# Five whole-tile slots filled by half-tile transfers, later stores, and a 512-column bias in a two-layer graph kernel

## The reference, cut to what matters

```python
# layer 0
x_norm = layernorm(x, g_in, b_in)
logits = x_norm @ Wn + bn;  gumbel = -log(-log(clip(u)) + EPS)
gate = straight_through(softmax(logits + gumbel))[:, 1]
view1 = x_norm
view2 = (adj * gate[:, None] * gate[None, :]) @ x_norm
g = sigmoid(concat([view1, view2], -1) @ Wg + bg)
fused = g * (view1 @ W1 + b1) + (1.0 - g) * (view2 @ W2 + b2)
x = layernorm(x + layernorm(fused + x, g_out, b_out))
# layer 1 (hyperbolic)
xt = logmap0(mobius_add(mobius_matvec(weight, x), expmap0(bias)))
h = adj @ xt
x = layernorm(x + hyperbolic_relu(h))
```

## Time and profile before

| | |
|---|---|
| median of 3 runs | 1006.14 us (1006.14 to 1008.36) |
| the profiled execution | 1008.98 us, span 1007.2 us |
| mean granted TensorE clock | 0.979 |
| busy, share of the span | PE 92%, DVE 79%, ACT 69%, GpSimd 22% |
| 16 DMA engines busy with the kernel's own queue | 75.4% |
| read from HBM, written | 271.37 MB, 9.46 MB |

### The profile page before, as it was taken

How to read it: one execution, slowest core, us unless ns; L and a number is a source line. 1 busy time by engine, 2 the same in 40 slices (tenths; PEclk the granted TensorE clock), 3 DMA queues, 4 the chain that set the end, 5 groups by cost and what they waited for, 6 DMA issues and landing times.

```text
span 1007.2 us, 12535 instructions
## 1 busy us (share of the span) xinstructions
PE 926.0 (92%) x4020; PEld 724.4 (72%) x4020; DVE 794.3 (79%) x1769; ACT 693.5 (69%) x1233; POOL 225.5 (22%) x201
## 2 busy tenths in 40 slices
PE   3888899999999999999999999998998988889983
PEld 2444677777878787878787887876777766668772
DVE  3555789888898979697784858669998887889984
ACT  4676476868686767656573654667878877778883
POOL 2220111121111111111010201002003716264552
PEclk8999999999999999999999999999999999999997
DMA  7677597977777677768584655758999897999890
GB/s 263 232 269 246 229 374 291 342 283 293 292 282 293 261 292 255 288 217 326 190 312 161 234 191 211 273 184 288 347 347 355 329 354 296 362 352 364 334 355 21
DMA packets 51537, 281.65 MB, mean 280 GB/s; under 512 B 6496, under 2 KB 8080, under 8 KB 20368
## 3 DMA queue, kind: packets, MB, share of 16 engines
q1 hardware_dynamic: 51472, 280.86, 75.4%
HBM read 271.37 MB, written 9.46 MB: 279 GB/s over the span
## 4 chain that ended last, share of the span: by engine, by line
PE 52%; DVE 20%; DMA 8%; ACT 8%; POOL 7%; issue 3%; SPq 1%; POOLq 0%; ACTq 0%; DVEq 0%
PE PS L982 15%; PE PS L984 15%; PE PS L983 15%; DMA A<-in_adjT_dram 6%; DVE AL L744 4%; DVE XGL L744 4%; DVE XTL L744 3%; PE PS L1066 2%; PE PS L1063 2%; DVE BS L693 2%; PE PS L980 1%; DMA xnt_scratch<-XNT 1%; ACT XGH L566 1%; POOL SINV L492 1%; ACT AH L566 1%
## 5 line engine op out<-in xcount | busy, mean ns | idle before, releaser
L744 DVE TENSOR_TENSOR AL<-A,AH 128x1024 fp32r<-128x1024 f32 x272 | 323.9, 1220 | 35.8 <-ACT AH L566 34.5
L566 ACT ACTIVATE AH<-A 128x1024 fp32r<-128x1024 f32 x272 | 277.2, 1057 | 88.8 <-PE PS L984 54.3
L982 PE MATMUL PS<-AH,XTH 128*128 128x512 f32 x326 | 131.7, 404 | 16.9 <-DVE AL L744 16.8
L982 PE MATMUL PS<-AH,XGH 128*128 128x512 f32 x364 | 145.4, 400 | 1.4 <-DVE AL L744 1.3
L984 PE MATMUL PS<-AH,XGL 128*128 128x512 f32 x364 | 141.8, 390 | 0.0
L983 PE MATMUL PS<-AL,XGH 128*128 128x512 f32 x364 | 141.7, 389 | 0.0
L744 DVE TENSOR_TENSOR XGL<-A,XGH 128x1024 fp32r<-128x1024 f32 x108 | 126.5, 1218 | 14.0 <-ACT XGH L566 13.8
L983 PE MATMUL PS<-AL,XTH 128*128 128x512 f32 x326 | 128.9, 395 | 0.0
L984 PE MATMUL PS<-AH,XTL 128*128 128x512 f32 x326 | 128.7, 395 | 0.0
L566 ACT ACTIVATE XGH<-A 128x1024 fp32r<-128x1024 f32 x108 | 107.9, 1053 | 17.4 <-DMA A<-in_adjT_dram 17.3
L469 POOL TENSOR_TENSOR r_rs<-r_v,NHALF 128x4 f32<-128x4 f32 x24 | 44.5, 1855 | 268.1 <-DVE r_v L699 268.1
(11 more groups left out here) (229 smaller groups left out, 1525.9 us busy)
## 6 DMA issues: line engine op xcount, KB each, us to landing
A<-in_adjT_dram SPq DMA_DIRECT2D x243, 1024.0 KB, 6.3
XR<-in_x_dram SPq DMA_DIRECT2D x16, 256.0 KB, 5.4
GB<-gate_scratch SPq DMA_DIRECT2D x12, 256.0 KB, 4.8
XNT<-xnt_scratch SPq DMA_DIRECT2D x12, 256.0 KB, 5.0
x_scratch<-X SPq DMA_DIRECT2D x12, 256.0 KB, 7.4
xnt_scratch<-XNT SPq DMA_DIRECT2D x6, 256.0 KB, 4.0
xnt_scratch<-X1T SPq DMA_DIRECT2D x6, 256.0 KB, 4.5
FU<-in_x_dram SPq DMA_DIRECT2D x4, 256.0 KB, 5.1
```

The lines of the kernel that those rows point to most:

```text
L566: a.activation(high(m), A[:, n % RING, h * HW:(h + 1) * HW], ACT.Copy).then_inc(S["hi"], 1)
L744: v.tensor_tensor(low(m), A[:, n % RING, h * HW:(h + 1) * HW], high(m).bitcast(F32), ALU.subtract).then_inc(S["lo"], 1)
L982: p.matmul(acc, hi[:, st], high(m)[:, mv], start=start, stop=False)
```

## The change

RING goes from 4 to 5 and SPLITS from 5 to 4. `load_a` moves each tile by two transfers of half a tile (4 KB in each partition), each half of a slot with a semaphore of its own (ld0a, ld0b, ...); the transfer of a half waits only for the same half of the slot's earlier tile, and ScalarE (TensorE for the unsplit tiles) waits for each half apart. The stores of results and the reloads of residuals move two tiles later in SyncE's queue. In the epilogue of layer 0 the columns are put in another order (V1 part first), the biases become 512 columns wide (a fourth part holds b1/2), and from row block 4 on view2 is no longer multiplied by -W2/2: the columns hold V1/2, the gate's argument and V2. VectorE computes (1 + tanh) * V1/2, (tanh - 1) * V2 and the difference of halves instead, which is one operation more.

```diff
-RING = 4
-SPLITS = 5
+RING = 5
+SPLITS = 4
+SUBTRACT_ON_DVE = 4
+STORE_AFTER = 15
+RELOAD_AFTER = 4
@@ load_a
-                if n >= RING:
-                    if n - RING in WHOLE:
-                        sp.wait_ge(S["used"], 2 * (n - RING + 1))
-                    else:
-                        sp.wait_ge(S["lo"], SPLIT_COUNT[2 * (n - RING) + 1])
                 row = (c * NCH + q) * P
-                sp.dma_start(A[:, n % RING, :], adjT[row:row + P, :]).then_inc(S[f"ld{n % RING}"], 16)
+                for h, name in enumerate("ab"):
+                    if n >= RING:
+                        if n - RING in WHOLE:
+                            sp.wait_ge(S["used"], 2 * (n - RING) + h + 1)
+                        else:
+                            sp.wait_ge(S["lo"], SPLIT_COUNT[2 * (n - RING) + h])
+                    sp.dma_start(A[:, n % RING, h * HW:(h + 1) * HW],
+                                 adjT[row:row + P, h * HW:(h + 1) * HW]).then_inc(S[f"ld{n % RING}{name}"], 16)
@@ start of the queue
-            for t, v in ((HB[:, :], b_hyp), (B3[:, 0:P], bg), (B3[:, P:2 * P], b1), (B3[:, 2 * P:3 * P], b2),
+            for t, v in ((HB[:, :], b_hyp), (B4[:, 0:P], b1), (B4[:, P:2 * P], bg), (B4[:, 2 * P:3 * P], b2), (B4[:, 3 * P:], b1),
                          (GOUT[:, :], g_out), (BOUT[:, :], b_out)):
@@ loop of the queue
                 for o, end in enumerate(ENDS):
-                    if n == end // 2 + 13:
+                    if n == end // 2 + STORE_AFTER:
                         store(o)
-                    if n == end // 2 + 2:
+                    if n == end // 2 + RELOAD_AFTER:
                         reload(o)
                 load_a(n)
@@ split_high
-                if h == 0:
-                    act.wait_ge(S[f"ld{n % RING}"], 16 * (n // RING + 1))
+                act.wait_ge(S[f"ld{n % RING}{'ab'[h]}"], 16 * (n // RING + 1))
@@ VectorE, fuse
+                    if front >= SUBTRACT_ON_DVE:
+                        link(v.scalar_tensor_tensor(out=v4(TH[:, :]), in0=v4(TH[:, :]), scalar=-1.0, in1=E[:, :, 2 * P:3 * P],
+                                                    op0=ALU.add, op1=ALU.mult))
+                        link(v.scalar_tensor_tensor(out=FU[:, :], in0=TH[:, :], scalar=-0.5, in1=FU[:, :],
+                                                    op0=ALU.mult, op1=ALU.add))
+                    else:
+                        link(v.tensor_tensor(v4(FU[:, :]), v4(FU[:, :]), E[:, :, 2 * P:3 * P], ALU.add))
@@ TensorE, l0
-                        p.matmul(E[:, t, 0:3 * P], ones[:, :], BP[:, :], start=True, stop=False)
+                        if front >= SUBTRACT_ON_DVE:
+                            p.matmul(E[:, t, P:3 * P], ones[:, :], BP[:, P:3 * P], start=True, stop=False)
+                            p.matmul(E[:, t, 0:P], ones[:, :], BP[:, 3 * P:], start=False, stop=False)
+                        else:
+                            p.matmul(E[:, t, 0:3 * P], ones[:, :], BP[:, 0:3 * P], start=True, stop=False)
                         p.matmul(E[:, t, 0:2 * P], XNT[:, blk(t)], RX[:, :], start=False, stop=False)
-                        last = p.matmul(E[:, t, 0:3 * P], GB[:, blk(t)], RS[:, :], start=False, stop=True)
+                        right = slice(P if front >= SUBTRACT_ON_DVE else 0, 3 * P)
+                        last = p.matmul(E[:, t, right], GB[:, blk(t)], RS[:, right], start=False, stop=True)
```

More of the change, by code:

```diff
@@ L163, in build @@
         BNB = sb("BNB", [P, 2])
-        BP = sb("BP", [P, 3 * P], BF16)
-        BR = sb("BR", [P, 3 * P], BF16)
+        BP = sb("BP", [P, CW], BF16)
+        BR = sb("BR", [P, CW], BF16)
         ones = sb("ones", [P, P], BF16)
@@ L168, in build @@
         NEG = sb("NEG", [P, BLK])
-        B3 = PART[:, 0, 0:3 * P]
+        B4 = PART[:, 0, :]
         WH = PART[:, 1, 0:P]
@@ L207, in build @@
         for name in (
-                "ld0", "ld1", "ld2", "ld3", "hi", "lo", "used",
+                "ld0a", "ld0b", "ld1a", "ld1b", "ld2a", "ld2b", "ld3a", "ld3b", "ld4a", "ld4b",
+                "hi", "lo", "used",
                 "xin0", "xin1", "xin2", "urow", "norm_vecs", "weights", "vecs", "const", "ident_ready",
@@ L379, in _ @@
             sp.dma_start(HBC[:, :], b_hyp.rearrange("(p o) -> p o", o=1)).then_inc(S["vecs"], 16)
-            for t, v in ((RX[:, 0:P], wg[0:P, :]), (RX[:, P:2 * P], w1), (RS[:, 0:P], wg[P:2 * P, :]),
-                         (RS[:, P:2 * P], w2), (RS[:, 2 * P:3 * P], w2), (WH, w_hyp)):
+            for t, v in ((RX[:, 0:P], w1), (RX[:, P:2 * P], wg[0:P, :]), (RS[:, 0:P], w2),
+                         (RS[:, P:2 * P], wg[P:2 * P, :]), (RS[:, 2 * P:3 * P], w2), (WH, w_hyp)):
                 sp.dma_start(t, v).then_inc(S["weights"], 16)
@@ L419, in _ @@
             for o, end in enumerate(ENDS):
-                if end // 2 + 2 >= NT:
+                if end // 2 + RELOAD_AFTER >= NT:
                     reload(o)
             for o, end in enumerate(ENDS):
-                if end // 2 + 13 >= NT:
+                if end // 2 + STORE_AFTER >= NT:
                     store(o)
@@ L569, in hyp_setup @@
                 if k == 1:
[L570 removed]
+                    act.wait_ge(S["vecs"], 128)
                     a.activation(JUNK[:, 0:P], HB[:, :], ACT.Square, accum_out=hbs[:, 0:1]).then_inc(S["hb_sq"], 1)
@@ L748, in prepare @@
                 dve.wait_ge(S["weights"], 16 * 6)
-                v.tensor_scalar(RX[:, P:2 * P], RX[:, P:2 * P], 0.5, None, ALU.mult)
-                v.tensor_scalar(RS[:, P:2 * P], RS[:, P:2 * P], -0.5, None, ALU.mult).then_inc(S["wt_scaled"], 1)
-                dve.wait_ge(S["vecs"], 112)
+                v.tensor_scalar(RX[:, 0:P], RX[:, 0:P], 0.5, None, ALU.mult)
+                v.tensor_scalar(RS[:, 0:P], RS[:, 0:P], -0.5, None, ALU.mult).then_inc(S["wt_scaled"], 1)
+                dve.wait_ge(S["vecs"], 128)
                 dve.wait_ge(S["const"], 1)
-                link(v.tensor_tensor(B3[:, P:2 * P], B3[:, P:2 * P], B3[:, 2 * P:3 * P], ALU.subtract))
-                link(v.tensor_scalar(B3[:, P:2 * P], B3[:, P:2 * P], 0.5, None, ALU.mult))
+                link(v.tensor_tensor(B4[:, 0:P], B4[:, 0:P], B4[:, 2 * P:3 * P], ALU.subtract))
+                v.tensor_scalar(B4[:, 0:P], B4[:, 0:P], 0.5, None, ALU.mult)
+                link(v.tensor_scalar(B4[:, 3 * P:], B4[:, 3 * P:], 0.5, None, ALU.mult))
                 for row in (0, 32):
-                    v.tensor_copy(BP[row:row + 1, :], B3[row:row + 1, :])
-                    link(v.tensor_copy(BR[:, :], B3[:, :]))
-                    link(v.tensor_tensor(B3[:, :], B3[:, :], BR[:, :], ALU.subtract))
-                v.tensor_copy(BP[64:65, :], B3[64:65, :]).then_inc(S["bias_ready"], 1)
+                    v.tensor_copy(BP[row:row + 1, :], B4[row:row + 1, :])
+                    link(v.tensor_copy(BR[:, :], B4[:, :]))
+                    link(v.tensor_tensor(B4[:, :], B4[:, :], BR[:, :], ALU.subtract))
+                v.tensor_copy(BP[64:65, :], B4[64:65, :]).then_inc(S["bias_ready"], 1)
             stats_pre(0)
@@ L839, in first @@
                     dve.wait_ge(S["tanh"], front + 1)
-                    link(v.scalar_tensor_tensor(out=v4(FU[:, :]), in0=v4(TH[:, :]), scalar=1.0,
-                                                in1=E[:, :, P:2 * P], op0=ALU.add, op1=ALU.mult))
-                    link(v.tensor_tensor(v4(FU[:, :]), v4(FU[:, :]), E[:, :, 2 * P:3 * P], ALU.add))
+                    link(v.scalar_tensor_tensor(out=v4(FU[:, :]), in0=v4(TH[:, :]), scalar=1.0, in1=E[:, :, 0:P],
+                                                op0=ALU.add, op1=ALU.mult))
+                    if front >= SUBTRACT_ON_DVE:
+                        link(v.scalar_tensor_tensor(out=v4(TH[:, :]), in0=v4(TH[:, :]), scalar=-1.0, in1=E[:, :, 2 * P:3 * P],
+                                                    op0=ALU.add, op1=ALU.mult))
+                        link(v.scalar_tensor_tensor(out=FU[:, :], in0=TH[:, :], scalar=-0.5, in1=FU[:, :],
+                                                    op0=ALU.mult, op1=ALU.add))
+                    else:
+                        link(v.tensor_tensor(v4(FU[:, :]), v4(FU[:, :]), E[:, :, 2 * P:3 * P], ALU.add))
                     if front >= ADD_ON_PE:
```

7 lines of the change are left out of this document (3 added, 4 removed).

## The result

The changed kernel takes **995.36 us** (median of 4 runs, 994.71 to 995.79) where the kernel before takes 1007.25 (1006.14 to 1009.46): a ratio of 0.9879, with a 95% interval of 0.9858 to 0.9899. That is faster, by 11.9 us or 1.2%. The forecast was 989 us in a range of 976 to 1001. The profiled execution took 994.71 us with a span of 992.9, 14.3 less than the profiled one of before; this is the pair that the forecast's sum of -17.2 is to be held against term by term. It flatters the change: the profiled execution of before is slower than its median, and that of the change is the fastest of its four. By the medians the forecast of 989 is 6.4 us too low.

What follows compares the result with a forecast made beforehand. The prediction took TensorE to bound 375 to 670 us, VectorE 670 to 750, and late loads behind store waits 750 to 981. Its terms summed to -17.2 us, giving 989 us from 1006.14, range 976 to 1001.

Steps and rivals of the forecast that it cites:

- The last stretch: 750 to 981 us: a DMA share of 0.965, smaller packets, earlier loads and less cover for GpSimd together give -9.9 us.
- Start: Start of the kernel: five more issues ahead of the first x_norm store delay ScalarE's next step, +1.2 us (0 to +2.4).
- Gate rows: Store of the gate rows: the load ahead of it waits for an earlier tile, -2.5 us (0 to -4.5).
- 110 to 375 us: Loads come sooner with five slots and halves, partly offset by fewer homes and load_front: -2 us (-5.5 to +2).
- Rival E: Row blocks 10 and 11: the missing home starves TensorE, some 30 us lost, slower at 1019 us; chance 0.05.
- Epilogue on TensorE: Row blocks 4 to 11: 128 fewer float32 columns per matmul, less 32 extra bf16 matmuls, -5.9 us (-3.3 to -6.8).
- Epilogue on VectorE: One more 512-column operation eight times, +0.7, and splits entering 670 to 750 us later, 1.2: +1.9 us (0 to +4).
- Homes from 375 us on: Row blocks 10 and 11 keep four homes; they refill while TensorE works on others: 0 us (0 to +5).
- B: Only TensorE's share comes; 750 to 981 us brings nothing: -7.3 us, 999 us; chance 0.17.
- C: 750 to 981 us reaches TensorE's limit, 25 us come back instead of 9.9: 974 us; chance 0.08.
- F: The whole kernel: the terms cancel within 3 us, 1006 us; chance 0.04.
- D: After 750 us small transfers lower the full-share DMA rate, deciding from 343 GB/s; 1016 us at 330; chance 0.04.

Runs made afterwards that it cites:

- experiment 2: The changed kernel with stores and reloads back at their old places in SyncE's queue, five slots and halves kept: 1000.16 us, ratio 0.9919.
- experiment 4: The changed kernel with four slots and five homes (RING = 4, SPLITS = 5), half transfers and late stores kept: 999.87 us, ratio 0.9918.
- experiment 6: The changed kernel with four slots (RING = 4) and its four homes, half transfers and late stores kept: 1004.98 us, ratio 0.9966.
- experiment 3: The changed kernel with one transfer and one semaphore for a whole tile, five slots and late stores kept: 996.52 us, ratio 0.9886.
- experiment 5: The kernel before with only stores and reloads moved two tiles later; four slots, five homes, whole transfers, old epilogue: 1005.45 us, ratio 0.9971.
- experiment 12: The changed kernel with four slots, five homes and the old places of stores and reloads; halves and 512-column epilogue kept: 1006.21 us, ratio 0.9969.
- experiment 1: The changed kernel with all 384 columns of the fp32 matmul back in every epilogue and no subtraction on VectorE: 998.4 us, ratio 0.9904.
- experiment 7: The changed kernel with load_front one tile later (k = 11 instead of 10), where it stood in time before: 993.5 us, ratio 0.9864.
- experiment 9: The changed kernel with early homes kept until row blocks 6, 8, 10 and 12 instead of 6, 6, 10 and 10: 991.34 us, ratio 0.9846.

## Why the prediction was right, and where it was not

The sign, the range and the place were right: most of the gain lies in the last stretch, and it comes from loads issued in time. Taken out of the change alone, the late stores cost 4.8 us there (experiment 2), the fifth slot 1.9 to 3.5 (experiments 4 and 6), the halves nothing (experiment 3). The sum was 2.9 us too good for the profiled pair, and that closeness is luck in part: the terms were 8.3 us too pessimistic in three places (gate rows, VectorE, last stretch) and 11.2 us too good in the others, the last half included. Term by term, by positions:

**The last stretch: forecast -9.9, measured -12.9, with 1.1 coming back in the last half.** The share I took, 0.965, came out at 0.96, the rate of a full share at 374 GB/s for 371, the packets at 8 ns for 9. What I had wrong is how the parts add. Gains of this stretch in the traces:

```
late stores alone                      -3.0   (experiment 5)
halves alone                           -5.4   (experiment 12)
halves and late stores, four homes     -9.3   (experiment 6)
halves and late stores, five homes    -11.0   (experiment 4)
halves and fifth slot, stores old      -8.1   (experiment 2)
fifth slot and late stores            -12.9   (experiment 3)
all                                   -12.9   (the change)
```

The forecast gave the halves 3.2 us of margin, the slot its own, the stores theirs, as if each was worth something in the presence of the others. Halves and late stores together are more than their sum, 11.0 against 8.4. As I read the waits, the chain needs both gone: halves alone leave 29.0 us of store waits, late stores alone leave ScalarE 25.6 us of waits for tiles, both leave 16.3. The difference of 2.6 us is larger than the 1.8 by which kernels with the same last part differ, but not by much. By the ratios late stores are worth 0.0051 with halves (experiments 12 and 4) and 0.0029 without (experiment 5), and their intervals do not part the two. The fifth slot with a home less adds 1.9; with four homes on either side (experiment 6) it adds 3.5. Once it is there, the halves add nothing. The last finding is against the title: the half-tile transfers are the part that this kernel could do without. All but its first row keep the 512-column epilogue; without it (experiment 1) the stretch gains 11.9, which lies within the 11.6 to 13.4 of the kernels that are alike there. The 1.1 of the last half stays open. It is there (1.1 to 1.3) in every run that gains 8 us or more in this stretch, with whole transfers too, and not in experiments 5 and 12.

**Start: forecast +1.2 (0 to +2.4), measured +2.9.** The step that failed is "Five issues more stand ahead", as the measure of the delay. Of the 2.9 us, 2.1 are there from half 2 to half 23. The store is issued 2.8 us later but takes 10.67 us instead of 11.74, so ScalarE goes on behind it at 28.95 us instead of 27.20. TensorE's group of eight after that takes 2.10 us at the lower clock, where the one of before took 1.31; the next half wins 0.4 back. The number of issues does not decide it: with whole transfers (experiment 3) one issue is added instead of five, ScalarE goes on at 28.81 us, and halves 2 to 23 are 2.5 us later. What holds the store back then stays open. The other 0.7 us come between halves 23 and 24, in every run with the wide biases and not in experiment 5: `prepare()` on VectorE, whose operations grew from 384 to 512 columns, runs from 90.11 to 94.67 us ahead of the next low splits, 4.56 us, where it took 3.83 before (87.98 to 91.81). The forecast had no term for it.

**Gate rows: forecast -2.5, measured -6.6.** The mechanism is the forecast's: a load ahead of the gate rows' store waits for an earlier tile. The store starts at 89.55 us instead of 90.82 and the first epilogue sooner. In order of time on VectorE and TensorE, against the earlier trace rows:

```profile
100.54 0.69 DVE L839 TENSOR_TENSOR GB<-PS,GB 128x512 f32<-128x512 f32 x1 [1.23 <-DMA XR<-in_x_dram]
...
101.58 0.34 PE L1078 MATMUL PS<-BP,ones 128*128 128x384 bf16 x1
```

TensorE has no idle time ahead of this epilogue where it had 4.52 us, and VectorE 1.23 where it had 6.26. From 90 to 110 us the share is 0.96 where it was 0.79, and TensorE busy for 16.50 us where it was 12.71. My bound of -4.5 counted only the wait. The term that it put at nothing is the clock behind the wait. The epilogue took 7.24 us before, its first half at the lower level:

```profile
103.65:107.40 3.75, 3.75 (x11) 2.64 (x12) 3.75 (x4) 0.00 (x0) 0.00 (x0) 0.55 0.34 90
```

With the change it takes 5.56 us:

```profile
101.58:107.10 5.52, 5.52 (x28) 4.13 (x28) 5.52 (x6) 0.00 (x0) 0.00 (x0) 1.00 0.99 367
```

These 1.7 us and the 4.5 of the wait are nearly all of the 6.3 us that lie between halves 26 and 27; halves 24 to 26 give the other 0.3.

**110 to 375 us: forecast -2 (-5.5 to +2), measured +2.7.** This is the worst miss, outside its bounds. The forecast said "there are 8 homes instead of 9", and then gave that no price. It did not say at all that from row block 6 on there are 6 instead of 7, which is where most of the loss lies. Experiment 6 puts the missing home at 4.1 us of position: 1.0 in row block 4, 2.1 in block 6 and 1.0 in block 7, behind half 168 and so outside this stretch. So 3.1 fall here. Experiment 7 puts `load_front` at 0.8 here. Against them stands 1.0 that experiment 4, with its five homes, gains here. Together that is +2.9 for the +2.7 measured. The -2 of the forecast was to come from earlier loads; no run shows that loads could have given it.

Rival E was this mechanism, at the wrong place: I looked for it in row blocks 10 and 11, where homes are fewest, and the positions lose nothing there. It bites in blocks 4, 6 and 7, before 385 us.

**Epilogue on TensorE: forecast -5.9, measured -3.1** by positions from 375 to 666 us (3.0 by the medians). The step that failed is "nearly all where TensorE never rests". Two of the eight epilogues, of row blocks 4 and 5, stand at 282 and 329 us, ahead of the full stretch, and the one of block 11 stands at its end. Five row blocks keep the gain; in 4 and 5 TensorE waits for splits, in 11 VectorE is last. By the forecast's own 0.183 per matmul the three are 2.2 us. And the extra bf16 matmul costs twice what I took, the other 0.6. The page of the Trainium skill that I weighed (TensorE: Matmul & The Clock Gate) gives 81 ns for it; the 0.06 us worked out above lies between that and my 0.03.

**Epilogue on VectorE: forecast +1.9, measured +0.7.** The operation is there with its 0.7 us. The 1.2 for the home at the transition is not: experiment 4, with five homes, shows the same +0.7.

**Homes from 375 us on: forecast 0, measured +0.9**, of which 1.0 falls in the first 30 us (experiment 1, which has the epilogue of before: -0.7 at half 168, +0.3 at 180, +0.2 at 288). It is the home that row block 7 lacks, and experiment 9 gives it back. After that, with every epilogue and all of row blocks 10 and 11 still to come, 0 as forecast. ScalarE waits longer for homes there, 72.9 us for 47.7 in the earlier trace rows, and TensorE notices nothing: surplus, as argued.

**The rivals.** B fell (the last stretch gained), C was never near, and F fell with 11.9 us by the medians. E was right in its mechanism and wrong in place and size, as said above. D, small transfers, fell at its point of decision: 374 GB/s at a full share, far above 343. The rule of the Trainium skill (DMA: Bandwidth & Descriptors, rules for kernel authors) on transfers of at least 1 MiB does not bind here; experiment 3 and the change differ by 1.2 us of 995 with twice the transfers. The 2 us of fixed cost that the prediction took from the same page of the Trainium skill (its section on the anatomy of one DMA) are fitted there to transfers issued from GpSimd, and these are SyncE's.

## What to carry to other kernels

Buffers, transfer size and the places of stores in an in-order queue all buy the same thing, a load that is issued in time: price them together, from the wait that would end last with the others in place, and after deepening a ring move whatever waits in its queue. Here the ring grew by one tile and the stores moved by two; one was not tried. Give a price to every resource that a change takes away, first of all in the stretches where the engine behind it has idle time. And read the first 30 us as carefully as the last 200: a new order of a store, two loads and the weights gave 6 us.

## What the runs showed that I had not expected

The store waits more than doubled, from 29.0 to 76.5 us, when the ring grew by a slot in place of a home and the stores stayed (experiments 12 and 2), and the kernel was still 6 us faster. A wait of 40 us in 150 at the head of `load_front` (experiment 7) was worth one or two microseconds. And 4.5 us of idle time of TensorE ahead of one epilogue cost 6.2: the engine then ran half of the epilogue at the lower clock.
